# Double norm buffers, listings in gaps and a later group table in a two-block kernel

## The reference, cut to what matters

```
h  = layernorm(x) * (1 + ca) + sa
x  = x + ga * attn(h)          # RWKV-like scan over 8 x 1024 tokens of 128, then a gelu feed-forward (128 -> 512 -> 128)
h  = layernorm(x) * (1 + cb) + sb
x  = x + gb * moe(h)           # 8 experts, top 2 of the gate's softmax
def moe(h):
    comb = top2(softmax(h @ Wg.T)), normalised
    for e in range(8):
        a, b = split(h @ W1[e].T + b1[e]);  g = a * sigmoid(b)
        out += (g @ Wo.T + bo) * comb[..., e]
```

## Time and profile before

| | us |
|---|---|
| median of 3 runs | 724.58 (724.09 to 725.37) |
| the profiled execution | 724.43 |
| its span, first to last instruction | 722.7 |
| attention block's last instruction on ACT ends | 483.47 |
| first expert group on PE | 498.66 |

### The profile page before, as it was taken

The page is one execution under the profiler, slowest core; times in us unless marked ns, Lnnn a source line. Parts: engine busy times, 40 slices in busy tenths (PEclk is TensorE's granted clock), DMA queues, the critical chain, the costliest instruction groups (busy, mean ns, idle before and its releaser), DMA issues. The chain is left out here.

```text
span 722.7 us, 14385 instructions
## 1 busy us (share of the span) xinstructions
PE 619.4 (86%) x3515; PEld 473.2 (65%) x3515; DVE 605.5 (84%) x1388; ACT 519.4 (72%) x1319; POOL 532.7 (74%) x653
## 2 busy tenths in 40 slices
PE   3667789999999989979889777626999999999994
PEld 1444557667777667657657566513888888888883
DVE  6389999999999999997999748437788888888884
ACT  2666578898888957987766676243787887788883
POOL 5456667899999779899969865366588766666666
PEclk9989999999999999999999999556999999999998
DMA  3998888889898897788787699625565444454530
GB/s 110 255 140 126 120 113 134 133 140 156 147 140 160 130 148 112 147 174 140 154 161 140 136 309 249 221 89 141 143 101 92 83 74 83 80 84 77 84 62 2
DMA packets 103301, 95.58 MB, mean 132 GB/s; under 512 B 14523, under 2 KB 82710, under 8 KB 102966
## 3 DMA queue, kind: packets, MB, share of 16 engines
q1 hardware_dynamic: 85846, 79.69, 59.1%
q0 software_dynamic: 16176, 12.75, 9.7%
q10 hardware_dynamic: 1200, 2.23, 0.8%
HBM read 35.47 MB, written 25.61 MB: 85 GB/s over the span
## 5 line engine op out<-in xcount | busy, mean ns | idle before, releaser
L2533 POOL DMA_INDIRECT out<-res,index x91 | 141.3, 1553 | 55.9 <-DVE res L2618 36.1
L899 POOL TENSOR_TENSOR rs_prod<-rT,state_rows 128x512 f32<-128x512 f32 x128 | 139.0, 1095 | 42.0 <-DVE state_rows L1861 40.2
L2457 ACT ACTIVATE sig<-ps_a 128x256 f32<-128x256 f32 x91 | 35.0, 384 | 42.7 <-PE ps_a L2363 25.7
L1472 PE MATMUL ps_f<-hnT_hi,mix_hi 128*128 128x512 f32 x128 | 55.7, 435 | 8.2 <-DVE hnT_lo L1938 7.1
L1510 PEld LDWEIGHTS ps_k<-w,gel 128*128 128x128 f32 x448 | 53.6, 198 | 12.2 <-issue 12.1
L2585 DVE SCALAR_TENSOR_TENSOR half<-ps_b,xg,sig 128x256 f32<-128x256 f32 x91 | 43.6, 479 | 20.4 <-ACT sig L2461 20.4
L1510 PE MATMUL ps_k<-w,gel 128*128 128x128 f32 x448 | 55.9, 284 | 0.3 <-ACT gel L1263 0.3
L2578 DVE SCALAR_TENSOR_TENSOR ps_a<-ps_a,xg,sig 128x256 f32<-128x256 f32 x91 | 44.4, 487 | 10.9 <-ACT sig L2457 10.8
L2483 ACT ACTIVATE ps_b<-bias_rows 128x512 f32 x89 | 53.0, 596 | 0.0
L1474 PE MATMUL ps_f<-hnT_hi,mix_lo 128*128 128x512 f32 x128 | 52.7, 412 | 0.0
L1473 PE MATMUL ps_f<-hnT_lo,mix_hi 128*128 128x512 f32 x128 | 52.7, 411 | 0.0
(11 more groups left out here) (399 smaller groups left out, 2021.6 us busy)
## 6 DMA issues: line engine op xcount, KB each, us to landing
v_spread<-vT SPq DMA_DIRECT2D x128, 256.0 KB, 6.2
xg<-sorted_scratch SPq DMA_DIRECT2D x91, 130.0 KB, 2.3
xin<-in_L_attn_x SPq DMA_DIRECT2D x16, 256.0 KB, 6.4
sorted_scratch<-gel SPq DMA_DIRECT2D x4, 910.0 KB, 8.5
x<-in_L_attn_x SPq DMA_DIRECT2D x14, 256.0 KB, 5.0
out<-x SPq DMA_DIRECT2D x14, 256.0 KB, 5.7
tokens_scratch<-h SPq DMA_DIRECT2D x12, 256.0 KB, 5.7
raw_w<-in_L_ffn_W ACTq DMA_DIRECT2D x2, 1024.0 KB, 14.7
```

What stands on the lines that cost most here:

```text
L899: pool.tensor_tensor(rs_prod[:, p, idx % 4], rT[p][:], state[idx][:, p * NT:(p + 1) * NT], ALU.mult).then_inc(s["rs_ready"], 1)
L1472: pe.matmul(dst[:], mix_hi[:, a, m, :], hnT_hi[p][:, cols_of], start=(a == NOW), stop=False)
L2533: pool.indirect_dma_start(out_rows, bass.IndirectOffsetOnAxis(ap=index[k % RESULTS][:, i:i + 1], axis=0), res[k % RESULTS][:, i, :], None, ...
```

## The change

It gives `shift4`, `ve4`, `rs4` and `mv4` a second buffer, so that `norm_root(t)` waits for the normalization of t - 2. On POOL the listings of batch 1 are spread between the roots, and gating of tile 12 goes to DVE. On SP `reload(13)` goes ahead of `stage_batch(1)`, `store_sum(12)` behind `spread_bias`, `load_bias_rows` ahead of `store_sum(13)`. On ACT the two halves of the raw expert weights are loaded later and apart. On PE and DVE the steps of the last tiles stand in another order; the head sums of tile 15 get a buffer of their own (`lora`). In the expert block all 20 steps of the late table stand inside the loop, behind both groups of pair 0, and the router's last steps come before `rest_pair(0)`.

```diff
-        st4, mv4, shift4 = sb("st4", [P, NQ, 6]), sb("mv4", [P, NQ, 2]), sb("shift4", [P, NQ])
-        ve4, rs4 = sb("ve4", [P, NQ]), sb("rs4", [P, NQ])
+        st4 = sb("st4", [P, NQ, 6])
+        mv4 = [sb(f"mv4{i}", [P, NQ, 2]) for i in range(2)]
+        norm4 = sb("norm4", [P, 2, 3, NQ])
+        shift4, ve4, rs4 = ([norm4[:, i, k] for i in range(2)] for k in range(3))
...
+        def heads_of(t):
+            return lora if t == LAST else o_sum
```

SP's drain:

```diff
                 reload(*at_tile(15))
+                reload(*at_tile(13))
                 stage_batch(1)
                 store_rows(11, 1)
-                store_sum(12, 0)
-                reload(*at_tile(13))
                 renew_late(12, 6)
                 load_last_rows()
                 spread_bias()
+                store_sum(12, 0)
+                load_bias_rows()
                 store_sum(13, 1)
-                load_bias_rows()
                 store_rows(12, 0)
```

POOL, in `norm_root` (`second_moments` on DVE changes `shift2_ready` of t - 1 to t - 2 likewise):

```diff
                 after(pool, s["ln2_mv"], t)
-                after(pool, s["xn4_ready"], t - 1)
+                after(pool, s["xn4_ready"], t - 2)
```

POOL's drain:

```diff
                 list_pair(1, 0)
-                gate_rows(*at_tile(12))
                 second_root(14)
                 list_pair(1, 1)
+                list_pair(1, 2)
                 second_root(15)
                 norm_root(12)
-                list_pair(1, 2)
+                list_pair(1, 3)
                 norm_root(13)
-                list_pair(1, 3)
                 list_pair(1, 4)
+                list_pair(1, 5)
                 norm_root(14)
+                list_pair(1, 6)
                 norm_root(15)
-                list_pair(1, 5)
-                list_pair(1, 6)
                 list_pair(1, 7)
                 list_last(0, FRONT_EARLY // 2)
```

ACT's drain:

```diff
                 normalize_second(11, 1)
-                load_experts()
+                load_out_w()
                 gelu(13, 3)
-                gelu(13, 2)
                 head_squares(15)
                 act.preload_act_table_set("natural_log_exp_and_others")
                 head_log(15)
                 head_root(15)
                 second_squares(14)
+                gelu(13, 2)
                 keep_rows(11)
                 second_scale(14)
                 keep_logits(11)
                 keep_second(14)
                 second_squares(15)
+                load_experts(0)
+                second_scale(15)
                 gelu(14, 1)
                 gelu(14, 0)
-                second_scale(15)
                 gelu(14, 3)
+                keep_second(15)
                 gelu(14, 2)
-                keep_second(15)
+                normalize_second(12, 0)
                 gelu(15, 1)
                 gelu(15, 0)
-                normalize_second(12, 0)
                 gelu(15, 3)
                 gelu(15, 2)
+                load_experts(1)
                 exps(2)
                 normalize_second(13, 1)
```

DVE's drain:

```diff
                 sum_heads(15, 1)
-                add_second(12)
                 add_heads(14)
                 better_root(15)
                 norm_heads(15)
                 gate_heads(15)
+                add_second(12)
+                gate_last(12, 6)
+                add_heads(15)
+                add_last(12, 0, 6)
...
                 second_moments(14)
+                weigh_shares(2)
+                scale_last(*at_tile(13))
+                find_offsets(2)
                 add_second(15)
```

DVE in the expert block (the ten calls of `late_table` stood before the loop):

```diff
+            def late_table():
+                dve.wait_ge(s["route_step"], Router.OFFSET)
+                table.late_sizes()
+                table.late_gaps()
+                table.before()
+                table.weigh_pairs()
+                table.pairs()
+                table.weigh_rows()
+                table.rows()
+                table.late_place()
+                table.class_ends()
+                table.step_back()
...
             tagger.tag(last_rows[:, RG:, TAGS:])
-            dve.wait_ge(s["route_step"], Router.OFFSET)
-            table.late_sizes()
...
-            table.late_place()
-            rest_pair(0)
             dve.wait_ge(s["ranks_ps"], 1)
             router.pick(ps_r[:, 0:RG * CLASSES].rearrange("p (g e) -> p g e", e=CLASSES))
             router.rows()
             router.whole_rows(dest[:, TILES * NQ - RG:])
-            table.class_ends()
-            table.step_back()
+            rest_pair(0)
             for k in range(PAIRS):
                 low_half(2 * k)
                 high_half(2 * k)
...
                     join(2 * k + 1)
+                if k == 0:
+                    late_table()
```

More of the change, by code:

```diff
@@ L1059, in norm_root @@
             def norm_root(t):
+                p = t % 2
                 after(pool, s["ln2_mv"], t)
-                after(pool, s["xn4_ready"], t - 1)
-                pool.tensor_scalar(shift4[:], mv4[:, :, 0], -1.0, 0.0, ALU.mult, ALU.add)
-                pool.tensor_scalar(ve4[:], mv4[:, :, 1], 1.0, EPS_LN, ALU.mult, ALU.add).then_inc(s["ln2_ve"], 1)
+                after(pool, s["xn4_ready"], t - 2)
+                pool.tensor_scalar(shift4[p][:], mv4[p][:, :, 0], -1.0, 0.0, ALU.mult, ALU.add)
+                pool.tensor_scalar(ve4[p][:], mv4[p][:, :, 1], 1.0, EPS_LN, ALU.mult, ALU.add).then_inc(s["ln2_ve"], 1)
                 after(pool, s["ln2_ve"], t)
-                pool.tensor_tensor(rs4[:], ve4[:], minus_half[:], ALU.pow).then_inc(s["ln2_rstd"], 1)
+                pool.tensor_tensor(rs4[p][:], ve4[p][:], minus_half[:], ALU.pow).then_inc(s["ln2_rstd"], 1)
                 after(pool, s["ln2_rstd"], t)
-                mean_shift(shift4, rs4, s["shift2_ready"])
+                mean_shift(shift4[p], rs4[p], s["shift2_ready"])
             def drain():
@@ L1282, in head_squares @@
                 after(act, s["o_ready"], t)
-                act.activation(o_sq[:], o_sum[:], ACT.Square).then_inc(s["osq_ready"], 1)
+                act.activation(o_sq[:], heads_of(t)[:], ACT.Square).then_inc(s["osq_ready"], 1)
             def head_log(t):
@@ L1372, in keep_small, with load_out_w, load_experts @@
                 act.activation(out_w[:], ps_k1[:, 0:NH2 * P].rearrange("p (h d) -> p h d", h=NH2), ACT.Copy).then_inc(s["small_ready"], 1)
-            def load_experts():
+            def load_out_w():
+                act.wait_ge(s["d_ready"], TILES)
+                act.dma_start(out_w_rows, ins["L0_ffn_Wo"]).then_inc(s["out_w_in"], 16)
+            def load_experts(i):
                 w_dram = ins["L0_ffn_W1"].rearrange("e (p c) d -> p e (c d)", c=CH)
@@ L1378, in load_experts @@
                 act.wait_ge(s["g_ps"], TILES)
[L1379 to L1382, removed]
+                act.dma_start(raw_w[:, i], w_dram[:, i * E // 2:(i + 1) * E // 2]).then_inc(s["expert_in"], 16)
             def spread_gates():
@@ L1581, in drain @@
                 score(10)
-                ffn2(12, 2, NQ)
+                spread_root(14)
+                reduce_odd(15, 1)
                 pe.wait_ge(s["scan_ready"], TILES * DK)
                 ffn1(13, 3)
[L1585 to L1588, removed]
                 join_heads(14)
@@ L1591, in drain @@
                 variance(15)
+                after(pe, s["gelu_ready"][1], 13)
+                ffn1(13, 2)
                 turn_rows(11, 1)
-                after(pe, s["gelu_ready"][0], 13)
-                ffn2(13, 0, 2)
                 spread_root(15)
+                ffn2(12, 2, NQ)
                 score(11)
-                ffn2(13, 2, NQ)
                 join_heads(15)
@@ L1600, in drain @@
                 turn_second(14)
+                after(pe, s["gelu_ready"][0], 13)
+                ffn2(13, 0, NQ)
                 await_second(14)
@@ L2060, in norm_heads @@
                 after(dve, s["rsg_ps"], t)
-                dve.scalar_tensor_tensor(out=ps_k1[:], in0=ps_k1[:], scalar=gn_half[:], in1=o_sum[:],
+                dve.scalar_tensor_tensor(out=ps_k1[:], in0=ps_k1[:], scalar=gn_half[:], in1=heads_of(t)[:],
                                          op0=ALU.mult, op1=ALU.mult).then_inc(s["onorm_ready"], 1)
@@ L2078, in sum_heads @@
                 after(dve, s["red_odd"], t)
-                after(dve, s["wo_ps"], t - 1)
-                dve.tensor_tensor(o_sum[:], ps_o[:], bonus[p][:], ALU.add).then_inc(s["o_ready"], 1)
+                if t < LAST:
+                    after(dve, s["wo_ps"], t - 1)
+                dve.tensor_tensor(heads_of(t)[:], ps_o[:], bonus[p][:], ALU.add).then_inc(s["o_ready"], 1)
             def rest_second(t):
@@ L2100, in second_moments @@
                 after(dve, s["ln2_stats"], t)
-                after(dve, s["shift2_ready"], t - 1)
-                token_moments(mv4, st4, s["ln2_mv"])
+                after(dve, s["shift2_ready"], t - 2)
+                token_moments(mv4[t % 2], st4, s["ln2_mv"])
             def find_first(r):
@@ L2170, in drain @@
                 add_last(13, 1, 6)
-                find_first(2)
+                find_second()
                 rest_second(15)
@@ L2174, in drain @@
```

(11 more changed lines are left out.)

9 lines of the change are left out of this document (3 added, 6 removed).

## The result

The changed kernel took 727.91 us (median of 20 runs, 722.95 to 732.3) against 723.69 us for the kernel before beside it (20 runs, 720.35 to 728.48). The ratio is 1.0054, 95% interval 1.0034 to 1.0074: 3.9 us slower (2.5 to 5.4). The forecast was slower, by 1.8 us.

The account below looks back on a forecast made before the run. PE's expert loop was taken to bound the kernel, gaining only by an earlier start and losing by holes. 724.43 - 3.3 (first block) + 3.5 (hole) + 1.6 (clock) = 726.2, against the median 726.4; 8-in-10 range 719.5 to 729.2 us.

Parts of the forecast that it names:

- The late table: Expert loop: the 4.4 us DVE block makes PE stand 3.5 us at group 4, then a clock dip costs 1.6.
- rival A: Loop at group 4: the hole is there but the clock level stays; 724.8 us, chance 0.18.
- The first block: Before the expert loop: 4.1 us gained, 0.8 lost to a later landing, sum -3.3 us.
- the double buffer takes away only the one on POOL: End of first block: of two waits in series, only POOL's at `norm_root(15)` goes; ACT's for the stored rows remains.
- the landing stays: First block: `store_rows(12)` lands within about a microsecond of now, taken as 0.8 us later, since the DMA engines are full.
- So the start moves from 473.80 to 469.69: ACT's `round_experts`: the wait for listings goes, gaining 4.11 us and no more.
- This is upstream of the same transfer and worth 0: Around 415 to 437 us: tile 12's gating on DVE and the head-sum buffer bring work forward 1 to 4 us, gaining 0.
- it costs nothing, but feeds nothing earlier either: POOL: `list_pair(1, 2)` ahead of `second_root(15)` waits for `stage_batch`, yet `second_root(15)` ends near 430.4 as now.
- The weights: First block transfers: both later halves (5.7 us) run before `store_rows(12)`, whose landing is taken as 0.8 us later.
- B: First block: `store_rows(12)` lands early, the chain moves by up to 12.4 us; 717.3 us, chance 0.22.
- D: Expert loop: the table does no harm, the first block's gain alone stays; 721.3 us, chance 0.08.
- C: First block: transfers get worse, late second weights half holds PE's `turn_experts(0, 2)`, or listings slow; up to 729.2 us, chance 0.12.

Follow-up runs that it names:

- e1: The kernel before with only the late table's 20 steps moved behind the second group of pair 0; 729.6 us against 726.11, ratio 1.0046.
- e7: The changed kernel with the late table's 20 steps run twice in the same place; 728.1 us against 722.16 for the kernel before, ratio 1.0088.
- e8: The changed kernel with the table's 20 steps in six pieces where DVE had idle time; 719.45 us against 722.16 for the kernel before, ratio 0.9967.
- e2: The changed kernel with the late table back ahead of the loop; 721.94 us against 726.11 for the kernel before, ratio 0.995.
- e4: e2 with `store_sum(13, 1)` and `store_rows(12, 0)` ahead of `load_bias_rows` on SyncE; 721.41 us against 726.11 for the kernel before, ratio 0.9934.
- e3: e2 with both raw weight transfers back at their earlier place behind `load_out_w`; 717.76 us against 722.16 for the kernel before, ratio 0.9928.
- e5: The kernel before with only double norm buffers and batch 1's listings moved ahead of the last norm root; 727.3 us against 726.11, ratio 1.0015.
- e10: e3 with SyncE's transfer order of the kernel before; 720.22 us against 726.67 for the kernel before, ratio 0.991.
- e6: The changed kernel run again, unaltered; 724.72 us against 722.16 for the kernel before, ratio 1.0028.

## Why the prediction was right, and where it was wrong

**The late table: right.** The block was to be 4.4 us, and is 4.44 (500.72 to 505.16). PE was to stand 3.5 us at group 4, and stands 3.11, 3.12 and 3.12. That the 20 steps in one block are the cause is shown three ways: alone they cost 3.3 us (e1), doubled they add 4.39 us of wait and about 4.3 us of time (e7), in pieces they cost nothing measurable (e8). The clock was to add 1.6. In the trace of after, 0.90 and 0.76 over two windows of 5 us make 3.4 us at the lower level, and so about 1.7 us lost where PE worked (an estimate from these rows). But the term is not constant: the clock fell after the hole in three of four traces (0.76, 0.66, 0.53) and stayed at 1.00 in e1, which is rival A. L to J is 213.4 to 216.4 us in the seven traces with the table ahead of the loop, mean 215.3, and 216.5, 219.0 and 219.4 with the block. The trace before happened to have the shortest of them, so its pair with after shows 5.6 us and the means 3.0. The medians say 3.3 in e1, and 5.7 to 7.5 between e2 and the changed kernel, on different chips; 5.1 was forecast, and they don't settle it closer. Nor do the parts add up: -3.6 (e2) and +3.3 (e1) make -0.3, where the changed kernel measured +3.9 and +2.0. The intervals just leave room for the 2.0 and not for the 3.9. Whether the two parts cost more together than apart, or the chips differ, stays open.

The Trainium skill ("TensorE: Matmul & The Clock Gate", section "HAM oscillation") has the engine throttled anew after each such wait for data in its loop. The traces agree in three of four; e1, with its 3.12 us, didn't show it.

**The first block: right in its sum, wrong in its parts.** The step "the double buffer takes away only the one on POOL" held: no long wait at `norm_root(15)`, no wait for listings. The step "the landing stays" held too: S to N moved by -0.6 us where I took +0.8, and within 2.1 us in every other kernel but e4. By the Trainium skill ("DMA: Bandwidth & Descriptors", section "Issuing engines are not separate DMA queues") transfers that different engines issue run on the same 16 DMA engines and interleave. The traces agree: with the weights early or late (e3, e2) the landing came 57.33 and 55.17 us after S, no further apart than in before and e1 (57.18 and 55.25), which are the same there. And e2 measured 3.6 us faster against 3.3 forecast. But two terms in it are mistaken, so that the sum came out is in part luck: in the trace of e2, N to O is 2.8 us longer than before and S to N 2.0 shorter, and neither was in the sum.

- "So the start moves from 473.80 to 469.69: 4.11 us gained, no more, since everything before it still starts from the normalization of tile 14." The start is the same, but the length of what follows is not fixed: N to O took from 6.91 to 12.50 us with the same instructions. In the trace of e5 this ate most of the gain, and the kernel measured 1.0015. In the changed kernel it took back 1.0 us.
- "This is upstream of the same transfer and worth 0", and of `list_pair(1, 2)` ahead of `second_root(15)`, "it costs nothing, but feeds nothing earlier either". The reordered queues are worth several us: e10 has only them and the buffers, and gains 0.9% (6.5 us) where the buffers with a smaller move of the listings gained nothing. They don't work through the transfer: in e3 it lands when it did (57.33 us after S), and in e10 nothing waits for it at N. In e10 and e3 they make the upstream work end later (`logits` of tile 12 at 453.76 in e3, 52.4 us after S, and at 448.08 before, 45.4 after S), PE is busy nearly up to the chain and goes on working in it, the clock is low for some 3 us only, and N to O is 2.0 to 2.5 us shorter.

**The weights.** I gave their new place a cost or gain only through the landing. What it does is to let the batch land early (POOL waits 2.10 us for it and not 8.36), so that the upstream work ends 9.5 us earlier than in e3 (`logits` of tile 12 at 444.23), long before it is needed, and PE idles: busy 4.72 of 12 us, clock 0.50. In the traces this undoes the short chain (10.40 against 6.91). The medians lean the same way, 0.995 with the weights late and 0.9928 early, but on different chips, and their intervals overlap; that this place costs time is read from the traces and not shown by the times.

**What stays open.** Which of the edits in POOL's, DVE's and PE's lists carries the gain wasn't tried one by one. The shorter N to O accounts for 2.0 to 2.5 of the 6.5 us of e10 and the vanished wait for 4; that these two are the whole of it is an argument from the traces, and in e10's own trace the gain is smaller (span 720.7 against 722.7 us). No run changed PE's work ahead of N and nothing else, so that this is what sets the clock in the chain is read from the traces and not shown. The wait of 3.6 us without a releaser in e2 and e5 isn't explained.

**The sum.** -3.3 and +5.1 gave +1.8; measured were +3.9 (2.5 to 5.4) and, on another chip, +2.0 (0.7 to 3.4). Rivals B and D didn't come: the landing stayed, and the table did harm. C didn't either; PE's wait for the second half of the weights was 2.37 us at 451.12, hidden before N.

## What to carry to other kernels

A block of short steps on an engine that feeds the bottleneck costs its length less the idle time that covers it, there and in the steps behind it (4.44 us of steps made a wait of 3.11), however small each step is; cut into pieces of two to five steps at the places where that engine waits anyway, the same work cost nothing measurable here. When a wait is hidden behind a transfer, work that ends earlier may only make TensorE idle longer before the chain that follows, and in most of these traces that chain then ran at the lower clock: try to let such work end just before it is needed. And price a chain behind a long wait by what TensorE does before it and between its parts, not only by its instructions.

## What the runs showed of the hardware

- With the same instructions, N to O took 6.91 to 7.66 us in the three traces of the table with weights early and new queues (PE busy 10.3 to 10.5 of the 12 us before, clock 0.78 to 0.92) and 9.0 to 12.5 in the others (clock 0.50 to 0.64). e4 (PE busy 10.01 us before, clock 0.62) has a wait of 2.54 us for a store in the chain, and there the clock fell behind N, when PE had stood 2.66 us.
- A short stand of PE was followed by the lower level: PE stood 1.52 us in e3 (until 455.25), and the clock was 0.51 from 456.3 to 459.6 us; it stood 1.53 us in e10 (until 457.07), and the clock was 0.50 from 459 to 462. Behind the stand of 3.12 us in e1 it stayed at 1.00.
- ACT's issue of half the weights took 0.39 and 0.37 us in the changed kernel, where I had taken 2; in the kernel before the same two issues took 2.34 and 1.79. SyncE's issue of `store_rows(12)`, 0.68 us before, took 9.20 in the changed kernel, with the DMA share at 0.98 meanwhile, and 7.8 to 9.7 in the others that have the weights late and SyncE's new order (e2, e6, e7, e8):

```profile
434.61 9.20 SPq L758 DMA_DIRECT2D state_rows<-h  x1
```

  Against S it was issued 6.3 us earlier than before and landed 0.6 us earlier.
